# Graph attention turned round: sources on the partitions, one exponential, sums from a column of ones

## The reference

```python
xn = layernorm(x)
x = x + graph_attention(xn) + linear_attention(xn)     # 4 heads of 256; 16 heads of 64
x = x + ffn(layernorm(x))                              # 1024 -> 512 -> 1024, fixed-point GELU

# graph_attention, with a self-loop at each node
xp = (xn @ W).reshape(N, 4, 256)
a_src, a_dst = einsum(xp, att_src), einsum(xp, att_dst)
e = leaky_relu(a_src[src] + a_dst[dst], 0.2)
alpha = exp(e - segment_max(e, dst)) / segment_sum(exp(e - ...), dst)
out = relu(segment_sum(xp[src] * alpha, dst) + bias)
```

## Time and profile before

| | |
|---|---|
| median of 3 runs | 3742.73 us (3742.1 to 3743.62) |
| profiled execution, its own time | 3739.34 us |
| span of the profile | 3737.7 us |
| mean granted TensorE clock | 0.969 of 2.4 GHz |
| busy: PE / VectorE / ScalarE / GpSimd | 92% / 75% / 42% / 25% |
| DMA over the span | 72 GB/s |

### The profile page before, as it was taken

The page is one execution under the profiler, slowest core; times in us unless marked ns, Lnnn a source line. Parts: engine busy times, 40 slices in busy tenths (PEclk is TensorE's granted clock), DMA queues, the critical chain, the costliest instruction groups (busy, mean ns, idle before and its releaser), DMA issues. The chain is left out here.

```text
span 3737.7 us, 52878 instructions
## 1 busy us (share of the span) xinstructions
PE 3444.8 (92%) x17197; PEld 2842.2 (76%) x17197; DVE 2799.8 (75%) x6375; ACT 1582.1 (42%) x2646; POOL 924.0 (25%) x564
## 2 busy tenths in 40 slices
PE   6899999979999968991999999999999999699998
PEld 5678888658888847771888888888888888577776
DVE  4577677667777744333988989889889898688886
ACT  2011111121111102111777777777777777354454
POOL 1266671057766775660000000000000000000000
PEclk8999999989999989995999999999999999899999
DMA  7833322334444433323011110110110110322221
GB/s 264 350 50 66 66 51 65 104 90 89 89 88 88 88 76 75 47 43 106 23 45 39 28 45 25 42 45 22 45 45 23 45 37 14 112 74 82 82 71 50
DMA packets 234863, 269.87 MB, mean 72 GB/s; under 512 B 177236, under 2 KB 177236, under 8 KB 231642
## 3 DMA queue, kind: packets, MB, share of 16 engines
q1 hardware_dynamic: 57741, 216.14, 19.0%
q0 software_dynamic: 173776, 40.24, 7.5%
q10 hardware_dynamic: 3250, 12.50, 0.9%
HBM read 177.03 MB, written 90.75 MB: 72 GB/s over the span
## 5 line engine op out<-in xcount | busy, mean ns | idle before, releaser
L1194 PE MATMUL G_acc<-values,G_probsT 125*125 125x256 f32 x5000 | 1165.0, 380 | 0.0
L1194 PEld LDWEIGHTS G_acc<-values,G_probsT 125*125 125x125 f32 x5000 | 901.9, 188 | 113.8 <-ACT G_probsT L1057 0.3
L317 POOL DMA_INDIRECT counts<-E_twins_now,E_cells_now x400 | 859.6, 2149 | 389.9 <-issue 252.6
L1030 ACT ACTIVATE G_probs<-G_asrc_row,G_shift 125x625 f32<-125x625 f32 x500 | 409.0, 818 | 384.6 <-PE G_tr L1178 284.2
L1102 DVE TENSOR_TENSOR G_probs<-G_probs,G_low 125x625 f32<-125x625 f32 x500 | 402.3, 805 | 99.9 <-issue 66.0
L1178 PEld LDWEIGHTS G_tr<-ident,G_probs 125*125 125x125 f32 x2500 | 339.5, 189 | 180.2 <-DVE G_probs L1104 160.6
L1178 PE MATMUL G_tr<-ident,G_probs 125*125 125x125 f32 x2500 | 369.7, 279 | 108.1 <-DVE G_probs L1104 103.4
L1104 DVE SCALAR_TENSOR_TENSOR G_probs<-G_probs,G_count 125x625 f32<-125x625 f32 x500 | 405.2, 810 | 17.3
L1035 ACT ACTIVATE G_low<-G_asrc_row,G_low_shift 125x625 f32<-125x625 f32 x500 | 407.5, 815 | 22.9 <-DVE G_probs L1102 22.6
L218 PE MATMUL V_v_ps<-V_w,V_xT 128*125 128x512 f32 x1200 | 281.4, 397 | 43.7 <-DVE V_xT L242 43.7
L218 PEld LDWEIGHTS V_v_ps<-V_w,V_xT 128*125 128x125 f32 x1200 | 224.2, 187 | 100.9 <-DVE V_xT L242 44.1
(11 more groups left out here) (169 smaller groups left out, 3943.1 us busy)
## 6 DMA issues: line engine op xcount, KB each, us to landing
counts<-K_zeros POOLq DMA_DIRECT2D x50, 763.5 KB, 8.3
G_count<-counts SPq DMA_DIRECT2D x25, 1367.2 KB
xnT<-K_xT_whole SPq DMA_DIRECT2D x25, 500.0 KB
Q_xT_whole<-xnT SPq DMA_DIRECT2D x25, 500.0 KB
V_xT_whole<-xnT SPq DMA_DIRECT2D x25, 500.0 KB
E_row<-edge_keys ACTq DMA_DIRECT2D x25, 488.3 KB
E_row<-edge_keys SPq DMA_DIRECT2D x25, 488.3 KB
K_rows<-in_x SPq DMA_DIRECT2D x25, 448.0 KB
```

Source lines behind the costliest of these rows:

```text
L317: nc.gpsimd.indirect_dma_start(out=counts_cells, out_offset=bass.IndirectOffsetOnAxis(ap=self.cells_now[:, slot, c:c + 1], axis=0), in_=se ...
L1030: nc.scalar.activation(probs[:, u % 4, :], asrc_row[:, h, s:s + UW], ACT.Exp, bias=shift[:, sl, h:h + 1]).then_inc(high_ready, 1)
L1194: m = nc.tensor.matmul(acc[0:T, h * C:(h + 1) * C], probsT[:, u % 2, b, :], values[:, t, h * C:(h + 1) * C], start=(t == 0), stop=(t == NT ...
```

## The change

The matrix is scattered turned: the key of an edge becomes `src * N + dst`, so a row of `counts` is a source. In G the sources now lie on the partitions, the destinations along the row, in groups of 7, 6, 6 and 6 tiles (875 or 750 destinations). A unit is a group and a head, 16 in all; a unit has 25 steps, one for each tile of sources, 400 in all. The blocks of weights are then already the stationary operand: no transpose and no copy out of PSUM. With `m = 0.8 a_src + (a_dst - top)` the leaky ReLU is a maximum ahead of one exponential: `exp(max(m, 0.2 a_dst - top) + 0.2 a_src)`. Each head's values get a 257th column of ones, so the matmul also makes the sums; the bias is added to `values` in V, where VectorE now does the copy out of PSUM. The maximum over neighbours is a running minimum of `absent - a_src` over the 25 steps of the unit two ahead (`nearest`), which is transposed and reduced, and the shifts go over DRAM to a row on every partition. The code of G is unrolled.

```diff
-                nc.vector.scalar_tensor_tensor(... in0=dst_c, scalar=float(N), in1=src_c, ...)
+                nc.vector.scalar_tensor_tensor(... in0=src_c, scalar=float(N), in1=dst_c, ...)
# graph_values
-                for cols in HALVES:
-                    nc.scalar.activation(values[...], v_ps[...], ACT.Copy)
+                    nc.vector.tensor_tensor(values[..., 0:C], v_ps[...], bias_row[...], ALU.add)   # two a tile
+            nc.gpsimd.memset(values[:, :, :, C:CW], 1.0).then_inc(ones_set, 1)
# graph_attention: RING 5, NEXT_RING 3, AHEAD 3, WEIGH_AHEAD 2; absent has 2 buffers
# SyncE
+            for k in range(STEPS):
+                u, j = k // NT, k % NT
+                if u + 2 < UN and not own_counts(u):      # own_counts(u): u % H < 2
+                    load_next(nexts_before(u) + j, u + 2, j)
+                if k + RING < STEPS:
+                    load_count(k + RING)
# GpSimd: broadcast(u + 1) (shifts to DRAM and back to a row on all partitions), store(u - 1) of gat
# ScalarE
+            def exponent(k):
+                act.wait_ge(raised_ready, k + 1)
+                nc.scalar.activation(here, here, ACT.Exp, bias=asrc_slope[...]).then_inc(exp_ready, 1)
+            for j in range(NT):
+                first_absences(j)
+            copy_shifts(0)
+            for k in range(AHEAD):
+                exponent(k)
+            for k in range(STEPS):
+                if u >= 1 and j == 0:
+                    for t in range(group(u - 1)):
+                        evacuate(u - 1, t)                # 125x257 out of PSUM
+                if k + AHEAD < STEPS:
+                    exponent(k + AHEAD)
+                if u + 2 < UN:
+                    absences_of_step(k)                   # Relu(1e30 - 1e30 count) -> absent
+                if u >= 1 and 8 <= j < 8 + group(u - 1):
+                    scale(u - 1, j - 8)                   # Relu(sums / total)
+                ...
# VectorE
+            def nearest(u, j, n_absent, n_least):
+                dve.wait_ge(absent_ready, n_absent + 1)
+                    dve.wait_ge(least_ready, n_least)
+                    nc.vector.scalar_tensor_tensor(out=here, in0=mask, scalar=term, in1=here,
+                                                   op0=ALU.subtract, op1=ALU.min).then_inc(least_ready, 1)
+            def lift(k):
+                    dve.wait_ge(multiplied, k - RING + 1)
+                nc.vector.scalar_tensor_tensor(out=weight[...], in0=rows[:, u % 2, 0, 0:w], scalar=asrc_most[...],
+                                               in1=rows[:, u % 2, 1, 0:w], op0=ALU.add, op1=ALU.max).then_inc(raised_ready, 1)
+            def weigh(k):
+                dve.wait_ge(exp_ready, k + 1)
+                dve.wait_ge(count_loaded[k % RING], 32 * (k // RING) + 32)
+                nc.vector.scalar_tensor_tensor(out=here, in0=here, scalar=1.0, in1=count[...],
+                                               op0=ALU.min, op1=ALU.mult).then_inc(weighted, 1)
+            for j in range(NT):
+                for u in range(2):
+                    nearest(u, j, j, 2 * j + u - 1)
+            floors(0, 0); floors(0, 1); shift(0)
+            for k in range(AHEAD):
+                lift(k)
+                if k < WEIGH_AHEAD:
+                    weigh(k)
+            for k in range(STEPS):
+                if k + AHEAD < STEPS:
+                    lift(k + AHEAD)
+                if u + 2 < UN:
+                    nearest(u + 2, j, absents_before(u) + j, least_steps(u + 2) + j)
+                if k + WEIGH_AHEAD < STEPS:
+                    weigh(k + WEIGH_AHEAD)
+                ...                                       # floors at j = 5 and 9, shift at j = 10, invert at j = 6
# TensorE
+            for k in range(STEPS):
+                pe.wait_ge(weighted, k + 1)
+                for t in range(group(u)):
+                    if j == 0 and u >= 1:
+                        pe.wait_ge(evacuated, min(banks_before(u - 1) + t + 1, banks_before(u)))
+                    m = nc.tensor.matmul(acc[0:T, t, 0:CW], weight[:, k % RING, t * T:(t + 1) * T], values[:, j, h, :],
+                                         start=(j == 0), stop=(j == NT - 1))
+                m.then_inc(multiplied, 1)
+                ...                                       # turn_least at j = 2 and 6, turn_shifts at j = 12
```

More of the change, by code:

```diff
@@ L86, in gps_layer @@
     gat_dram = nc.dram_tensor("gat", (N, D), F32).ap()
-    asrc_dram = nc.dram_tensor("asrc", (H * N,), F32).ap()
+    shift_dram = nc.dram_tensor("shifts", (2, 2 * WIDEST), F32).ap()
     outer = ExitStack()
@@ L992, in unit @@
-    def unit(u, slot):
-        return (u % UN) // UC, (u % UC) * UW, (slot + u // UN) % 2
+    RING, NEXT_RING = 5, 3
+    count = sb("count", [T, RING, WIDEST])
+    weight = sb("weight", [T, RING, WIDEST])
+    next_count = sb("next_count", [T, NEXT_RING, WIDEST])
+    absent = sb("absent", [T, 2, WIDEST], BF16)
+    least = sb("least", [T, 2, WIDEST])
+    rows = sb("rows", [T, 2, 2, WIDEST])
+    sums = sb("sums", [T, max(GROUPS), CW])
+    inverse = sb("inverse", [T, max(GROUPS)])
+    asrc_most, asrc_slope = sb("asrc_most", [T, H, NT]), sb("asrc_slope", [T, H, NT])
@@ new lines, in graph_attention, with group, at, width @@
+    scaled, gat_stored, link = sem("scaled"), sem("gat_stored"), sem("link")
+    ABSENT = 1.0e30
+    AHEAD, WEIGH_AHEAD = 3, 2
+    STEPS = UN * NT
+    def group(u):
+        return GROUPS[u // H]
+    def at(u):
+        return GROUP_AT[u // H]
+    def width(u):
+        return group(u) * T
+    def banks_before(u):
+        return sum(group(v) for v in range(u))
+    def cells(u, j):
+        return a["counts_rows"][j * T:(j + 1) * T, at(u) * T:at(u) * T + width(u)]
+    def own_counts(u):
+        return u % H < 2
@@ L996, in graph_attention, with nexts_before, least_steps, absents_before @@
+    def nexts_before(u):
+        return NT + sum(NT for v in range(u) if v + 2 < UN and not own_counts(v))
+    def least_steps(u):
+        return NT * u
+    def absents_before(u):
+        return NT + sum(NT for v in range(u) if v + 2 < UN)
     with nc.Block() as block:
@@ L1008, in _ @@
[L1008 to L1018, removed]
@@ L1021, in _ @@
         @block.scalar
         def _(act):
[L1023 to L1057, removed]
-                    if more:
-                        act.wait_ge(joined, g * UN + u + 2)
-                        low_branch(u + 3, slot)
@@ L1065, in _ @@
+            for t in range(group(UN - 1)):
+                evacuate(UN - 1, t)
+            for t in range(group(UN - 1)):
+                scale(UN - 1, t)
         @block.vector
         def _(dve):
-            dve.wait_ge(terms_turned, 1)
-            nc.vector.tensor_copy(aT[:, :], aps[0:H * NT, 0:T]).then_inc(terms_copied, 1)
             chain = Chain(dve, link)
-            chain.step(nc.vector.memset(top[:, :], 0.0))
-            def absences(slot, c):
-                chain.settle()
-                chain.step(nc.vector.tensor_scalar(absent[:, :], count[:, slot, c * UW:(c + 1) * UW], 0.0, NEVER,
-                                                   ALU.is_equal, ALU.mult))
@@ new lines, in weigh, with invert @@
+            def weigh(k):
+                u = k // NT
+                here = weight[:, k % RING, 0:width(u)]
+                dve.wait_ge(exp_ready, k + 1)
+                dve.wait_ge(count_loaded[k % RING], 32 * (k // RING) + 32)
+                nc.vector.scalar_tensor_tensor(out=here, in0=here, scalar=1.0, in1=count[:, k % RING, 0:width(u)],
+                                               op0=ALU.min, op1=ALU.mult).then_inc(weighted, 1)
+            def invert(u):
+                n = group(u)
+                dve.wait_ge(evacuated, banks_before(u + 1))
+                if u >= 1:
+                    dve.wait_ge(scaled, banks_before(u))
+                nc.vector.reciprocal(inverse[:, 0:n], sums[:, 0:n, C]).then_inc(inverse_ready, 1)
```

378 lines of the change are left out of this document (214 added, 164 removed).

## The result

| | before | changed |
|---|---|---|
| median, us | 3742.41 (3740.32 to 3743.62, 4 runs) | 4136.76 (4135.23 to 4146.93, 4 runs) |
| profiled span, us | 3737.7 | 4133.7 |
| mean granted TensorE clock | 0.969 | 0.943 |

The changed kernel is slower: the ratio is 1.106, 95% interval 1.1041 to 1.1079. The forecast was 4138 us.

What follows compares the result with a forecast made beforehand. Before, TensorE bounds G; changed, a serial ScalarE-VectorE chain does. G's terms 1784 + 1635 + 28 + 137 + 10 = 3594, against 3198: +396 us, so 4138 us; range 4080 to 4260, upper end 4290 for late loads or scatter.

Steps and rivals of the forecast that it cites:

- The serial chain: G's mask-making steps: lift, exponent, absences, nearest, weigh run one after another, 4.53 us a step at 750 columns.
- The order on ScalarE: G: strict FIFO keeps absences behind the exponent that waits for lift; step 4.5 us, or 2.8 if it could pass.
- What bounds the last two units: G's units 14 and 15, without nearest or mask: TensorE bounds, 49 steps x 2.79 = 137 us.
- The start: G before its first iteration: first masks and minima, store, broadcast, first lifts; 87 us after 1697, at 1784.
- The loop: G's 350 steps that make masks: 1635 us of chained steps, plus 28 us of VectorE's small work.
- VectorE's small work: G: reduces, short instructions and a reciprocal are not hidden, about 1.9 us in each of 15 units, 28 us.
- The end: From G's last matmul to F: last copies, scalings and GpSimd's stores, 10 us where it was 4.5.
- the scatter: Q and V: scattering over all of counts taken as 0 us; bounds +90 and 15 us below.
- the evacuations and scalings in ScalarE's gap: G's unit edges: hidden in ScalarE's 2.7 us idle per step; uncovered, evacuations would cost 30 us in all.
- Overlapping steps: Rival in G: masks run a step ahead and TensorE bounds, 3505 us in all; chance 0.06.
- TensorE's clock: Rival in G: clock falls to 1.2 GHz, a step takes 5.6 or 6.5 us, 4662 us in all; chance 0.05.
- Loads: Rival: count loads in G (+60 us) or the scatter (+90) bound, 4198 to 4288 us; chance 0.09.

Runs made afterwards that it cites:

- e1: Changed kernel with ScalarE's two instructions of an iteration swapped, mask ahead of the exponential: 3544.8 us, 0.9488 of the kernel before.
- e2: Changed kernel with VectorE's weigh ahead of nearest, ScalarE's order kept: 3842.09 us.
- e3: Changed kernel with lifts 4 and weighs 3 steps ahead instead of 3 and 2, same ring of 5: 4133.65 us.
- e4: Changed kernel with about half of TensorE's products in G left out: 4106.22 us.
- e7: Changed kernel with the old edge key (destination * N + source), so the matrix is scattered as before: 4135.58 us.

## Why the prediction was right

*The serial chain.* Shown, by e1 (cut it: -592 us), e2 (one link out of it: -295), e3 (lead: nothing) and e4 (half of TensorE's work: nothing in the loop). The step was put at 4.53 us and is 4.56. Two parts of this sum were off and cancelled, which is luck: without the first of them it would have been 4.47 us, and the loop 31 us short. I added 0.06 us for extra semaphore waits; the timeline shows handovers of 0.02 to 0.04 us with two waits in front, so the waits cost nothing that shows. And lift and nearest, with a column of per-partition scalars, take 0.994 and 1.001 us where weigh, with a constant, takes 0.933. I had sized all three by forms with a constant, 0.94. The two longer forms add about 0.11 us. (Whether the column of scalars makes them longer was not tested; their inputs differ too.)

*The order on ScalarE.* In the changed kernel ScalarE waits for a load of counts 8 times in the whole loop, 14.4 us together (the row below), so at nearly every step the mask's operand is there, and still it starts 0.83 us after the exponential, which waits 2.44 us for lift; moved ahead of it in the program (e1) it runs early. The Trainium skill, "TensorE: Matmul & The Clock Gate", beside its queue depths, calls ScalarE strict FIFO; the trace and e1 agree. From the waits of the changed kernel, 1776 to 3440:

```profile
ACT G_absent L1102 <- DMA G_next_count<-counts: 14.4, 8, 3.7
```

*What bounds the last two units.* TensorE, as said, but at 2.60 us a step, not 2.79. By the prediction's own list (products of 0.23 us) this term was wrong: back to back an instruction of 257 columns takes 0.217 us, 96.37 us for 444 in the changed kernel. The 0.233 of the earlier trace rows is the same pace and the run-out of the last instruction of each ten, under which the transposes already start: ten take 2.32 us in the kernel before, and the transposes begin 2.17 us after the first. From the changed kernel, then the kernel before:

```profile
3486.95 96.37 PE L1308 MATMUL G_acc<-values,G_weight 125*125 125x257 f32 x444
```

```profile
2304.12 2.32 PE L1194 MATMUL G_acc<-values,G_probsT 125*125 125x256 f32 x10
2306.29 0.71 PE L1178 MATMUL G_tr<-ident,G_probs 125*125 125x125 f32 x5
```

TensorE itself began step 350 at 3450.6, after a wait of 4.74 us at the edge of unit 14, so one step more than counted was left. From 3452.0 to the last product's end at 3583.3 is 131 us for 137.

*The start.* The first lift of the loop was put at 1784 and came at 1776.8. Of this 3.3 us is G's earlier start, which is chance: the other profiles have it anywhere up to 1703.9. The first rounds of two nearest came 3.2 to 3.5 us apart, then 2.09, so the 25 took about what was forecast; the store took 2.0 us instead of 5, and the broadcast landed after 6.1 instead of 9.

*The loop.* From the first lift at 1776.8 to the lift of iteration 350, the first with no mask in front, at 3452.0 is 1675 us; 1635 + 28 was the sum. The 12 us more are mostly the 0.02 or 0.03 us by which each of the 350 steps is longer. The 28 us for VectorE's small work came out by luck: in a unit with no late load it adds 1.2 us, not 1.9 (unit 4 takes 115.2 us, 25 steps of 4.56 are 114.0), and late loads and the edges between groups filled the rest.

*The end.* 12 us from the last matmul to F, for 10. Summed: 1776.8 + 1675 + 131 + 12 = 3595, for 3594. The terms were 7 us early and 6 us short on one side and 12 and 2 us long on the other, and cancel. The mechanism was right; that the total meets the median within 2 us is luck.

*Priced at nothing and right:* the scatter (e7), the evacuations and scalings in ScalarE's gap (2.44 us of gap left in a step with a scaling, 0.92 us in one with seven evacuations), the adds in V. On the scatter one reading was off: late in Q a batch of 500 edges lies over nearer 50 rows than 16, an estimate from how the reference draws the destinations. e7 settles the matter without it.

*The rivals.* Overlapping steps (0.06): false of this kernel, but e1 is that rival made real: 3544.8 us against the 3505 worked out for it, and VectorE, not TensorE, bounds its loop. TensorE's clock (0.05): it fell in part of the steps, below, but rose again soon enough: the slow step shown there took 4.50 us of the chain's 4.56, and in the whole loop VectorE waited for masks alone, never for TensorE. In e4 TensorE stayed mostly low, and its half of the work still fitted. Loads (0.09): not in the changed kernel, where they are those 14.4 us; in e1 they cost 70 us.

## What to carry to other kernels

A balance of busy times says what a loop could reach, not what it will: write both engines' programs of one iteration side by side and follow who waits for whom. If A's second instruction waits for B's second, and B's first waits for A's first, then all four are serial. A longer lead didn't change that here (e3), and a deeper ring can't, by the same argument, though none was run on this kernel. Put the instruction whose inputs are ready ahead of the one that waits for this iteration's work. And to tell a chain from a busy engine, take out one link: a chain gives back its length in each step (0.85 us for weigh), a hidden engine nothing (half of TensorE's products). After the cut, ask again who bounds: the busiest engine by share of the window was TensorE, and the one with no idle but for its masks was VectorE.

## What the hardware showed that was not expected

TensorE's clock did not hold at full. The forecast took 1.00 from one stretch of 16 us. In the changed kernel's loop the mean is 0.93. At 750 columns single steps ran at the lower of the clock's two levels. The windows of one such step and the next:

```profile
2804.00:2809.00 5.00, 4.46 (x13) 3.22 (x13) 3.13 (x8) 2.13 (x3) 0.00 (x0) 0.66 0.26 72
2809.00:2814.00 5.00, 3.06 (x14) 2.17 (x12) 3.20 (x4) 2.13 (x3) 0.00 (x0) 1.00 0.31 88
```

The timeline of the products around it, and the reduce of VectorE that lies in front of a lift there:

```profile
2799.65 2.87 PE L1308 MATMUL G_acc<-values,G_weight 125*125 125x257 f32 x12 [1.70 <-DVE G_weight L1237]
2804.54 4.50 PE L1308 MATMUL G_acc<-values,G_weight 125*125 125x257 f32 x12 [2.02 <-DVE G_weight L1237]
```

```profile
2799.51 0.41 DVE L1203 TENSOR_REDUCE G_floor<-G_tr 125x2 f32<-125x250 f32 x1
2799.84 0.99 DVE L1228 SCALAR_TENSOR_TENSOR G_weight<-G_rows,G_asrc_most 125x750 f32<-125x750 f32 x1
```

The slow step starts 4.89 us after the last instead of 4.56: a short reduce put lift back by 0.33 us, and with it the ring. TensorE had been idle 2.02 us instead of 1.70 ahead of it, and its 12 instructions took 4.50 us instead of 2.87. The next step started late too, behind the shifts' four short instructions, but after only 0.45 us of idling, and ran at full clock. At half the products (e4) it stayed near the lower level, 0.57. At 875 columns it was more: over long stretches of units 0 and 1 every second step ran at the lower level, 4.99 us for 3.30. There the same 1.86 us of idling lay ahead of steps at either level:

```profile
1802.32 3.30 PE L1308 MATMUL G_acc<-values,G_weight 125*125 125x257 f32 x14 [1.86 <-DVE G_weight L1237]
1855.50 4.99 PE L1308 MATMUL G_acc<-values,G_weight 125*125 125x257 f32 x14 [1.86 <-DVE G_weight L1237]
1860.66 3.30 PE L1308 MATMUL G_acc<-values,G_weight 125*125 125x257 f32 x14 [0.17 <-DVE G_weight L1237]
```

So the idle time just ahead does not by itself say which level a step gets, and what does stays open. A stage in which such steps were on the path would pay 1.6 to 1.7 us for each.
